# Set-up of a two-layer graph network: weight transfers on SyncE's queue, table clearing first on ScalarE's, and the first scatter into each table written without adding

## The reference

```python
# layer 0
feat_neigh = segment_sum(edge_val[:, None] * feat_in[edge_col], edge_row, n)
out = branch(feat_in, W_self, b_self, ...) + branch(feat_neigh, W_neigh, b_neigh, ...)
x = layernorm(x + out)
# layer 1: gather f[edge_src], weight it by a small MLP of edge_scalars, segment_sum
# to edge_dst, small matrices W_l2_*, an angle from W_l3_*, cos / sin mixing
x = layernorm(x + out1)
```

## Time and profile before

| What | Value |
|---|---|
| median of 3 runs | 5481.23 us |
| the runs | 5476.78, 5481.23 and 11055.83 us |
| profiled execution | 5474.58 us, span 5472.8 us |
| busy share of the span | PE 64%, DVE 50%, ACT 48%, POOL 74% |
| set-up block | 0 to about 57 us |
| first scatter to last | 105.9 to 3043.4 us |

### The profile page before, as it was taken

The page is one execution under the profiler, slowest core; times in us unless marked ns, Lnnn a source line. Parts: engine busy times, 40 slices in busy tenths (PEclk is TensorE's granted clock), DMA queues, the critical chain, the costliest instruction groups (busy, mean ns, idle before and its releaser), DMA issues. The chain is left out here.

```text
span 5472.8 us, 83484 instructions
## 1 busy us (share of the span) xinstructions
PE 3514.5 (64%) x18421; PEld 2921.1 (53%) x18421; DVE 2741.4 (50%) x11176; ACT 2617.3 (48%) x9201; POOL 4066.4 (74%) x3277
## 2 busy tenths in 40 slices
PE   3555555555555555555555376888888888888872
PEld 2333333443333343333433245888888888888871
DVE  4555556555655655565555384333333333333338
ACT  1222222222222222222222256888888888888863
POOL 1788888888888888888888555777777777777750
PEclk9677766666666676777676577777777777777775
DMA  7666666666666666666665783333333333333323
GB/s 257 109 111 111 119 113 111 112 112 111 112 118 113 111 112 114 113 112 117 111 112 95 144 196 101 81 79 81 82 79 81 81 79 81 81 79 81 79 74 128
DMA packets 698443, 588.07 MB, mean 107 GB/s; under 512 B 286734, under 2 KB 566184, under 8 KB 695325
## 3 DMA queue, kind: packets, MB, share of 16 engines
q0 software_dynamic: 286576, 224.93, 29.7%
q1 hardware_dynamic: 396280, 310.47, 20.3%
q10 hardware_dynamic: 15542, 52.19, 2.4%
HBM read 374.64 MB, written 212.60 MB: 107 GB/s over the span
## 5 line engine op out<-in xcount | busy, mean ns | idle before, releaser
L709 POOL DMA_INDIRECT sums_scratch<-vals,to_i x1568 | 2446.5, 1560 | 593.7 <-issue 375.0
L996 POOL DMA_INDIRECT fg<-f_scratch,src_e x1568 | 1486.2, 948 | 499.6 <-issue 477.3
L617 PE MATMUL ps_n<-same,hot 128*40 128x128 f32 x3136 | 693.9, 414 | 1349.2 <-issue 1349.2
L1049 ACT ACTIVATE hot<-raw,e_s 128x40 f32<-128x40 f32 x6272 | 1392.3, 313 | 343.7 <-DVE raw L1072 318.0
L617 PEld LDWEIGHTS ps_n<-same,hot 128*40 128x40 f32 x3136 | 557.8, 185 | 1457.9 <-issue 1394.1
L660 ACT COPY near<-ps_n 40x512 f32<-40x512 f32 x196 | 113.5, 579 | 1666.3 <-PE ps_n L617 1666.3
L1025 PE MATMUL ps_eu<-hot,prod 128*128 128x120 f32 x3136 | 891.0, 378 | 0.0
L1078 DVE TENSOR_TENSOR prod<-ps_ew,fg 128x256 f32<-128x256 f32 x392 | 164.4, 419 | 1237.8 <-DMA fg<-f_scratch,src_e 1237.8
L1023 PEld LDWEIGHTS ps_eu<-hot,prod 128*128 128x128 f32 x3136 | 623.1, 244 | 300.8 <-DVE prod L1079 213.5
L1023 PE MATMUL ps_eu<-hot,prod 128*128 128x40 f32 x3136 | 619.2, 288 | 244.5 <-DVE prod L1079 244.0
L1025 PEld LDWEIGHTS ps_eu<-hot,prod 128*128 128x128 f32 x3136 | 621.4, 246 | 0.0
(11 more groups left out here) (189 smaller groups left out, 3812.0 us busy)
## 6 DMA issues: line engine op xcount, KB each, us to landing
srow_s<-in_src SPq DMA_DIRECT2D x196, 512.0 KB
e_s<-in_edge_attr SPq DMA_DIRECT2D x196, 256.0 KB, 3.8
hid_scratch<-hid SPq DMA_DIRECT2D x196, 256.0 KB, 3.8
hid_e<-hid_scratch SPq DMA_DIRECT2D x196, 256.0 KB
sums_scratch<-zeros ACTq DMA_DIRECT2D x24, 1056.0 KB, 20.8
sums_scratch<-vals,to_i POOLq DMA_INDIRECT x1568, 3.4
fg<-f_scratch,src_e POOLq DMA_INDIRECT x1568
t_in<-sums_scratch POOLq DMA_DIRECT2D x72, 256.0 KB, 6.7
```

The costliest lines, as they stand in the source:

```text
L617: last = pe.matmul(ps_n[t // TH][:, t % TH, :], hot[:, k, t, :], same[:, k, t, :], start=True, stop=True)
L709: pool.indirect_dma_start(out=sums_d[i], out_offset=bass.IndirectOffsetOnAxis(ap=to_i[:, j, t:t + 1], axis=0), in_=vals[:, j, t, :], in_of ...
L996: pool.indirect_dma_start(out=fg[:, j, t, :], out_offset=None, in_=f_d, in_offset=bass.IndirectOffsetOnAxis(ap=src_s[:, j, t:t + 1], axis= ...
L1049: last = act.activation(hot[:, k, t, c, :], raw[:, k, t, :], ACT.Copy, scale=e4_s[:, j, t, c:c + 1])
```

## The change

The 26 weight transfers move from ScalarE's queue to SyncE's. SyncE now waits for the zeroed tiles (`zeroed`, 5), issues the 26, and only then waits for `attr_z` and issues the two transfers of `attr_r`. ScalarE's queue begins with the 24 clearing transfers, which wait only for the memset of `zeros`. The first scatter into each table (`n == 0`) writes its rows (`ALU.bypass`) and doesn't add; every table is still cleared before, and the wait for that stays.

```diff
@@ SyncE, set-up block
-                    sp.wait_ge(attr_z, 1)
-                    sp.dma_start(attr_r[0:NB - 1, :, :].rearrange("b p c -> b (p c)"),
-                                 a["node_vec1"][0:(NB - 1) * BN].rearrange("(b n) o -> b (n o)", b=NB - 1)).then_inc(wts_in, 16)
-                    sp.dma_start(attr_r[NB - 1:NB, 0:PLAST, :].rearrange("b p c -> b (p c)"),
-                                 a["node_vec1"][(NB - 1) * BN:N].rearrange("(b n) o -> b (n o)", b=1)).then_inc(wts_in, 16)
-
-                @block.scalar
-                def _(act):
-
-                    act.wait_ge(zeroed, 5)
+                    sp.wait_ge(zeroed, 5)
                     n = 0
 
                     def put(to, fro):
                         nonlocal n
-                        act.dma_start(to, fro).then_inc(blk_in, 16)
+                        sp.dma_start(to, fro).then_inc(blk_in, 16)
                         n += 16
...
                     assert n == 16 * 26
+                    sp.wait_ge(attr_z, 1)
+                    sp.dma_start(attr_r[0:NB - 1, :, :].rearrange("b p c -> b (p c)"),
+                                 a["node_vec1"][0:(NB - 1) * BN].rearrange("(b n) o -> b (n o)", b=NB - 1)).then_inc(wts_in, 16)
+                    sp.dma_start(attr_r[NB - 1:NB, 0:PLAST, :].rearrange("b p c -> b (p c)"),
+                                 a["node_vec1"][(NB - 1) * BN:N].rearrange("(b n) o -> b (n o)", b=1)).then_inc(wts_in, 16)
+
+                @block.scalar
+                def _(act):
+
+
                     act.wait_ge(z_set, 1)
                     for i in range(NTAB):
                         for z in range(ZSPLIT):
@@ GpSimd, scatter stage
                                 settle(pool, n_scat if t == TS - 1 else passed)
+                                first = isinstance(n, int) and n == 0
                                 pool.indirect_dma_start(
                                     out=sums_d[i], out_offset=bass.IndirectOffsetOnAxis(ap=to_i[:, j, t:t + 1], axis=0),
-                                    in_=vals[:, j, t, :], in_offset=None, compute_op=ALU.add).then_inc(added[i], 16)
+                                    in_=vals[:, j, t, :], in_offset=None,
+                                    compute_op=ALU.bypass if first else ALU.add).then_inc(added[i], 16)
```

## The result

The changed kernel took 5512.74 us (median of 6 runs, 5502.17 to 5517.3) against 5479.73 us (median of 6, lowest 5473.31, one of them 11055.83) before: the ratio is 1.006, with a 95% interval of 1.0046 to 1.0074. Forecast was 5466 us, in a range of 5453 to 5486 us. So it is 0.6% or 33 us slower, small but clear, and on the other side. The profiled execution has a span of 5512.6 us, 39.8 us more than before; the 6.8 us between the two differences are within what single executions of one kernel differ by.

What follows compares the result with a forecast made beforehand. GpSimd was taken as the bound, running scatters back to back, so the stage's end follows its first scatter. First load -9.5, `e64_s` -1.4 and plain scatters -1 sum to -11.9 us: forecast 5466 us, range 5453 to 5486 us.

Steps and rivals of the forecast that it cites:

- Clearing first on ScalarE: Set-up: clearing issued from about 3.2 us, ScalarE through at 41.9 us, clearing traffic over at 69.3 us against 83 us.
- Weights on SyncE: Set-up: 26 weight issues slowed under the clearing, 0.55 + 0.76 us each; SyncE through at 40.5 us (32 to 50).
- issue decides: SyncE in set-up: issuing, through at 40.5 us, sets the pace, nearly tied with draining its packets by 37.6 us.
- `attr_r` behind the weights: Set-up: `attr_r` there at 44.5 us, then TensorE and VectorE; VectorE ends last in the block at 52.5 us (44 to 62).
- First load: Start of scatter stage: issued at 57 us, there at about 71 us against 80.53 us, -9.5 us.
- `e64_s`: First group of scatter stage: this load lands within a microsecond or two of the first three, -1.4 us (0 to -1.6).
- The plain first scatters: Scatter stage: four of 1568 scatters may land sooner or build faster; -1 us taken, +0.3 us at the other end.
- The second one: Rival, set-up: SyncE's queue becomes the bound at 3 us an issue, first load at 109 us, 5503 us; chance 0.10.
- the third: Rival, scatter stage: first scatter 10 to 12 us earlier but gain not seen in the end, 5474 to 5484 us; chance 0.15.
- The sign of the failure: Scatter stage: forecast wrong if the last scatter, expected at 3030 to 3034 us, doesn't follow the first.
- The 0.60 MB: Start of scatter stage: amount moved in 2 us at 84 to 86 us; a set of loads has no more to move.
- a block that ends at 44 us: Low case of the set-up block's end: full 15 us of interleaving end at 68.5 us, first load -12 us.

Runs made afterwards that it cites:

- e_plain: Only the four plain (`ALU.bypass`) first scatters, put into the kernel before, with its set-up; 5523.59 us against 5477.97 us, ratio 1.008.
- e_queues: Changed kernel with every scatter adding, only the queues exchanged; 5469.7 us against 5477.97 us before, repeated (_b) 5468.62 us against 5480.06 us.
- e_attr_b: Exchanged queues, all scatters adding, `attr_r` put back ahead of the weights on SyncE, second run; 5467.87 us against 5480.06 us before, ratio 0.9976.
- e_late2: Kernel before with only the first two scatters of the third group plain, behind 16 adding ones; 6474.7 us against 6455.2 us before.
- e_end2: Kernel before with only the last two scatters of the last group plain; 6472.2 us against 6467.7 us before, repeated 5505.74 us against 5480.06 us.
- e_last: Kernel before plus one plain scatter of 128 rows in the last stage, behind all scatters and gathers; 6484.7 us against 6483.1 us before.

## Why the prediction was wrong

*Clearing first on ScalarE*, right: issue from 3.08 to 43.1 us (forecast 3.2 to 41.9).

*Weights on SyncE*, right in mechanism and size: issues of 1.1 to 1.3 us, through at 38.6 us (forecast 40.5). Where both queues have work they get about as many packets each, as this stretch of the changed kernel shows (60 to 64 us):

```profile
q10 hardware_dynamic: 209, 1.57, 96.0%
q1 hardware_dynamic: 216, 0.06, 6.5%
```

While the weights are issued (20 to 30 us) SyncE gets fewer, which fits the "issue decides" of the working: its queue had no more to send.

```profile
q10 hardware_dynamic: 561, 4.20, 99.5%
q1 hardware_dynamic: 386, 0.03, 2.7%
```

*`attr_r` behind the weights*, right: TensorE at 43.4 us, VectorE through at 51.2 us (44.5 and 52.5). *First load*: 70.91 us (71), -9.6 us where -9.5 stood. It was issued at 54.66 us in place of 57; as the working said, that hardly moves it, for ScalarE's packets of zeros end near 70 us (69.3) in any case. *`e64_s`*: TensorE starts 4.07 us behind VectorE where it was 5.52 us, -1.45 us (-1.4). The first scatter, 11.4 us earlier at 94.52 us, is inside 93 to 96 us.

*The plain first scatters* is the step that failed. It said "Four of 1568", took -1 us for them, weighed their own build and landing, and ended its range at "+0.3 us for a form used for the first time". For the four themselves it was about right: they take 1.23 and 0.98 us in the first pair where the earlier trace rows has 1.84 us for the first, and the second scatter into table 0 starts 4.84 us behind the first in place of 6.45 us, 1.6 us won; the four adding ones behind that pair take 1.59 to 1.97 us in place of 1.54, which gives 0.7 us back. Its error was to take the duration of all other scatters and gathers for fixed, without a reason. In the mean they grew by 21 and 10 ns (the medians by 20 and 8), which on the one engine that has no slack in these stages is 33 and 16 us. `e_plain` shows the term alone: +45.6 us where -1 us stood. With that term taken out, `e_queues` and `e_queues_b` give 8.3 and 11.4 us against a sum of -10.9 us: the rest of the working holds.

No rival foresaw it. The second one, slower by SyncE's queue, has the sign and not the cause; the third, that the start's gain isn't seen in the end, names the stage in which it went but for another reason. The sign of the failure was among those listed: the last scatter, at 3064.9 us where 3030 to 3034 stood, doesn't follow the first.

Three slips of the working changed nothing in the sum. Of the four issues under load that the earlier trace rows show, two and not three are at 1.0 to 1.2 us; the others are 0.40 and 3.84 us. The 0.60 MB is enough for the first three loads of a group, but all six are some 0.8 MB (4, 512, 4, 2 x 20 and 256 KB). And for a block that ends at 44 us its own steps (4.4 us, 4 us and the full 15 us) give 67.4 us for the first load, not 68.5; `e_attr_b`, with the block's end at 45.1 us, had it at 67.58 us.

What stays open is the cause of the longer durations. Shown is that they go with another form of transfer in the scatter stage (eleven kernels have one and all are longer; six have none, the kernel before included, and none of them is longer, the one with a plain scatter in the last stage among them). Shown is also that memsets don't do it, that neither the number of plain ones nor the number of changes between forms gives the size, that a step can be seen at the plain pair (`e_late2`), and that the longer level can also be there ahead of it (`e_end2`, twice). No run shows what in GpSimd takes the 6 to 20 ns, and nothing here explains why `e_end2` is longer from its first scatters on.

## What to carry to other kernels

On an engine that runs back to back through thousands of like instructions, price an edit by what it may do to all of them: 10 ns on 1568, 15.7 us, are more than the 11.4 us that the whole set-up gained. Don't mix forms of GpSimd transfers in its hot stage for the sake of a handful of cheaper ones, and compare the median duration of the untouched instructions after such an edit. A large clearing that others must share the DMA engines with is worth issuing early: here it held back the first load by its packets, to 80.53 us, long after its issue was over at 57 us. The version to keep is the exchange of the queues with adding scatters, 5468.6 us against 5480.1 us before; the whole change took 5512.7 us against 5479.7.

## What the runs showed of the hardware that was not expected

- A plain scatter of 128 rows mostly held GpSimd for 0.96 to 0.99 us (single ones up to 1.30 us), an adding one 1.54 us. Four plain ones in place of adding ones save 448 packets (286576 before, 286128 after), 112 each; the one that `e_last` adds brings 32.
- Another form of transfer in GpSimd's scatter stage went with longer adding scatters there and longer gathers in a later stage. One plain scatter, gather or direct load gave 1552, 1559 and 1548 ns in place of 1542, and 955 ns a gather in place of 944 to 947; the four plain ones of the change gave 1562 and 952 ns. One memset or eight did nothing.
- With both queues full, SyncE and ScalarE got equally many packets however unequal in size: 214 each in 4 us before (0.00 and 1.66 MB), 216 and 209 after (0.06 and 1.57 MB).
